# Three of four convolution chunks on TensorE in the first batch, with new planner lengths and ranks

## The reference, cut to what matters

```
x = x + 0.5 * ffn0(layernorm(x))      # shared weight plus 8 low-rank experts of rank 16
x = x + mamba2(layernorm(x) * w + b)
x = x + 0.5 * ffn0(layernorm(x))
x = x + 0.5 * moe(layernorm(x))       # 8 experts, top 2, and a shared expert of width 352
x = x + attention(layernorm(x))       # 16 heads of 8, linear attention over a batch
x = x + 0.5 * moe(layernorm(x))
```

```
xBC = u @ W_xbc.T                      # 512 channels: 256 of x, 128 of B, 128 of C
xBC = silu(conv4(xBC) + conv_b)        # each channel by itself, over time
```

## Time and profile before

| | |
|---|---|
| median of 3 runs | 946.68 us |
| lowest and highest | 939.96 and 947.03 us |
| the profiled execution, its own time | 947.6 us |
| span of that execution | 946.3 us |
| busy PE / PEld / DVE / ACT / POOL | 87 / 67 / 59 / 61 / 56 % |
| mean granted TensorE clock | 0.949 of full speed |

### The profile page before, as it was taken

One profiled execution on the slowest core, in us unless ns is written; L12 is line 12 of the kernel. 1 busy time (PEld: TensorE's weight loads), 2 busy tenths in 40 slices (PEclk: granted clock), 3 DMA queues, 4 the chain that ended last, 5 costly groups with the idle time before them and its releaser, 6 DMA issues.

```text
span 946.3 us, 15952 instructions
## 1 busy us (share of the span) xinstructions
PE 827.4 (87%) x4890; PEld 635.9 (67%) x4890; DVE 556.3 (59%) x1900; ACT 572.7 (61%) x1335; POOL 529.2 (56%) x648
## 2 busy tenths in 40 slices
PE   7999999999999987999789878987997895995983
PEld 6668688587776676686666667756666662764762
DVE  5487687877475757578546455598773461461113
ACT  4899787479877776786356335753743552552451
POOL 4058252586345787166753656565475665555453
PEclk9999998999999999999899899998997996998997
DMA  9920000010100012001131113121111421321323
GB/s 301 413 97 1 1 1 2 32 49 13 29 24 12 30 49 82 12 23 35 55 105 39 45 46 113 45 82 55 51 43 43 131 65 56 91 82 47 102 69 115
DMA packets 55652, 63.50 MB, mean 67 GB/s; under 512 B 7483, under 2 KB 47419, under 8 KB 55355
## 3 DMA queue, kind: packets, MB, share of 16 engines
q1 hardware_dynamic: 45299, 41.21, 14.2%
q0 software_dynamic: 9984, 20.60, 6.7%
q10 hardware_dynamic: 288, 0.67, 0.2%
HBM read 27.53 MB, written 34.92 MB: 66 GB/s over the span
## 4 chain that ended last, share of the span: by engine, by line
PE 48%; issue 14%; DVE 11%; POOL 11%; ACT 7%; DMA 6%; another core or an unknown queue 3%; SPq 0%; POOLq 0%; DVEq 0%; ACTq 0%
PE psum L529 8%; PE psum L800 7%; PE psum L820 6%; POOL sorted_x L1718 5%; PE psum L609 4%; PE psum L749 3%; PE psum L734 3%; PE psum L739 3%; DMA sent_y<-e_y,e_sx 2%; POOL sent_y L1728 2%; DMA e_sx<-sorted_x 2%; PE psum L678 2%; PE psum L842 2%; PE psum L524 1%
## 5 line engine op out<-in xcount | busy, mean ns | idle before, releaser
L1728 POOL DMA_INDIRECT sent_y<-e_y,e_sx x184 | 182.9, 994 | 156.1 <-ACT e_y L1557 111.4
L1718 POOL DMA_INDIRECT sorted_x<-g_xn,r_slot x128 | 129.0, 1008 | 38.6 <-issue 32.8
L800 PE MATMUL psum<-gu_w,e_sx 128*128 x368 | 129.4, 479 | 5.6 <-issue 3.5
L1252 DVE TENSOR_TENSOR e_h<-e_h,psum 128x352 f32<-128x352 f32 x96 | 47.8, 502 | 140.7 <-ACT e_h L1549 94.1
L820 PE MATMUL psum<-d_w,e_h 88*128 x736 | 104.5, 288 | 17.8 <-issue 13.7
L820 PEld LDWEIGHTS psum<-d_w,e_h 88*128 88x128 f32 x736 | 95.3, 200 | 34.8 <-issue 33.4
L1557 ACT ACTIVATE e_y<-psum,e_sx 128x128 f32<-128x128 f32 x184 | 57.5, 362 | 96.6 <-PE psum L820 57.2
L800 PEld LDWEIGHTS psum<-gu_w,e_sx 128*128 128x128 f32 x368 | 65.8, 197 | 34.9 <-issue 15.4
L1375 ACT ACTIVATE e_h<-psum 88x512 f32<-88x512 f32 x96 | 54.5, 572 | 48.0 <-PE psum L529 29.7
L1549 ACT ACTIVATE e_h<-psum 128x352 f32<-128x352 f32 x96 | 42.8, 450 | 62.5 <-PE psum L800 40.9
L529 PE MATMUL psum<-w_ffn,e_h 128*88 128x128 f32 x368 | 58.1, 283 | 20.8 <-issue 12.0
(11 more groups left out here) (241 smaller groups left out, 1933.0 us busy)
## 6 DMA issues: line engine op xcount, KB each, us to landing
e_sx<-sorted_x SPq DMA_DIRECT2D x88, 130.0 KB
sorted_x<-c_ys SPq DMA_DIRECT2D x8, 975.0 KB, 20.2
c_ys<-sent_y SPq DMA_DIRECT2D x14, 512.0 KB
sorted_x<-c_ys SPq DMA_DIRECT2D x8, 520.0 KB, 19.9
sent_y<-e_y,e_sx POOLq DMA_INDIRECT x184
xs<-in_x SPq DMA_DIRECT2D x8, 256.0 KB, 7.5
sorted_x<-g_xn,r_slot POOLq DMA_INDIRECT x128
out<-xs SPq DMA_DIRECT2D x7, 256.0 KB
```

The costliest lines, as they stand in the source:

```text
L800: last = e.matmul(two.banks[j].tile[:, 0:2 * IEXP], e_xT[k % SXS][:, j, :], gu_w[:, bass.ds(which[j] * (2 * IEXP), 2 * IEXP)], start=True, ...
L1718: e.indirect_dma_start(out=sorted_x[g], out_offset=bass.IndirectOffsetOnAxis(ap=r_slot[n][:, k, t:t + 1], axis=0), in_=rows[:, j, :], in_o ...
L1728: e.indirect_dma_start(out=sent_y[g], out_offset=bass.IndirectOffsetOnAxis(ap=e_sx[k % SXS][:, j, DM:DM + 1].bitcast(U32), axis=0), in_=e_ ...
```

## The change

Three things change together:

- `FOLDED` gets a third chunk for the first batch: chunks 1, 2 and 3 are folded there, and chunk 0 alone is tapped. The second batch stays as it was. `SCALED` follows and becomes (1, 2, 3), so one more DMA of 256 KB and one more multiplication on POOL prepare weights, and `w_gates` and the blocks of x behind it are loaded one place later in SP's queue.
- The planner counts a vector or scalar stage's engine as free 0.1 us earlier (`NEXT`), and thirteen lengths are replaced. For DVE all are shorter (for example the softplus series 3.67 to 2.8, taps 2.5 to 2.34); for POOL some are longer (the first half of four scatters 2.5 to 3.1, `finish` 1.29 to 1.6, two of `attn_out` 1.23 to 1.38); the issue of an expert load on SP 0.0 to 0.45.
- All rank lists are replaced.

```
-FOLDED = [(2, 3), (2, 3)]
+FOLDED = [(1, 2, 3), (2, 3)]
...
-FIRST = [177.82, 370.46, -25.93, -76.55, -165.11, 314.87, 71.46, 191.43]
+FIRST = [-1663.69, 1119.95, 260.62, 1433.81, -1495.37, 743.05, 409.58, 805.66]
...
-MAMBA = [-220.03, -96.33, 78.29, 264.38, -151.98, 471.11, 141.78, 20.16]
+MAMBA = [-1091.27, -162.89, 560.01, -466.1, -949.04, 507.42, 426.99, -1390.6]
...
-SORTED = [-32.7, 164.91, 159.92, 469.36, 679.99, 79.15, -248.93, 706.41]
-PAIRED = [114.03, 309.91, 329.73, 75.24, 663.43, 51.59, 642.15, 1319.33]
-PACE = [2.96, 5.27, 20.02, 6.49, 13.67, 17.1, 42.71, -15.01]
-SENDS = [576.11, 347.38, 560.08, 395.87, 1181.36, 460.83, 487.46, 1487.3]
+SORTED = [-580.11, -261.2, 560.37, -272.79, 299.31, -202.37, -1606.16, 1687.4]
+PAIRED = [220.41, 565.43, -75.92, -140.36, 1682.82, -653.42, 1054.59, 2350.85]
+PACE = [45.42, 98.75, 23.17, 108.81, -6.17, 12.68, 138.97, 28.74]
+SENDS = [236.06, 1496.96, 2345.51, -219.19, 999.47, 1264.13, 605.9, 1540.16]
...
-LATENCY, PE_LATENCY, TRANSFER, TABLE = 0.12, 0.25, 2.2, 1.3
+LATENCY, PE_LATENCY, TRANSFER, TABLE, NEXT = 0.12, 0.25, 2.2, 1.3, 0.1
...
-        free[name] = begin + course.cost
+        signals.now = begin + course.cost
+        free[name] = signals.now - (NEXT if name in ("vector", "scalar") else 0.0)
...
-                yield T + 14.0, 3.67, ("m_spexp", b + 1), ("a_exp", 1)
+                yield T + 14.0, 2.8, ("m_spexp", b + 1), ("a_exp", 1)
...
-                    yield T + 15.0 + TAP_STEP * n, 2.5, ("m_conv", k), ("m_tap", k + 1), ("m_halo_in", k + 1)
+                    yield T + 15.0 + TAP_STEP * n, 2.34, ("m_conv", k), ("m_tap", k + 1), ("m_halo_in", k + 1)
...
-                        yield (T + 8.0 + 4.0 * nth + 2.0 * half, 2.5, ("r_slot", g + 1), ("g_xn", i + 1), ("zeros", 16 * sum(EMPTY_LOADS)),
+                        yield (T + 8.0 + 4.0 * nth + 2.0 * half, 2.5 if half else 3.1, ("r_slot", g + 1), ("g_xn", i + 1), ("zeros", 16 * sum(EMPTY_LOADS)),
...
-                yield PAIR[g][t], 0.0, *scattered(g), before
+                yield PAIR[g][t], 0.45, *scattered(g), before
```

More of the change, by code:

```diff
@@ L87 @@
 ATANH = [2.0 / (2 * k + 1) for k in range(8)]
-FIRST = [177.82, 370.46, -25.93, -76.55, -165.11, 314.87, 71.46, 191.43]
-AGAIN = [135.09, -90.43, 35.89, -371.33, 70.69, 179.13, 111.78, 168.67]
-MAMBA = [-220.03, -96.33, 78.29, 264.38, -151.98, 471.11, 141.78, 20.16]
-CHUNK_AT = [24.78, 17.98, 107.37, 30.64, 119.59, 76.35, 60.04, 58.75]
+FIRST = [-1663.69, 1119.95, 260.62, 1433.81, -1495.37, 743.05, 409.58, 805.66]
+AGAIN = [775.72, -382.68, 554.79, -2296.04, -248.07, 248.47, 568.69, 223.34]
+MAMBA = [-1091.27, -162.89, 560.01, -466.1, -949.04, 507.42, 426.99, -1390.6]
+CHUNK_AT = [400.02, -213.35, 599.68, -252.35, -624.39, -851.15, 324.95, -1145.46]
 GAP = 4.9
@@ L277, in weave @@
             signals.late, free[name] = PE_LATENCY, clock.run(begin, course.cost)
-        signals.now = free[name]
+            signals.now = free[name]
         if not course.go_on():
@@ L790, in experts @@
                     numbers(g, 0)
-                yield T + 5.5, 1.28, ("two", 1), ("e_down", k - 1), ("w_late", 16 * 3), ("e_xT", k + 1)
+                yield T + 5.5, 1.21, ("two", 1), ("e_down", k - 1), ("w_late", 16 * 3), ("e_xT", k + 1)
                 on.wait_ge("w_late", 16 * 3)
@@ L981, in mamba @@
                 row = lambda k: dtt[:, k, :]
-                yield T, 1.8, ("f0_res", FFN0_AT[0, b] + 1), ("m_sum", b - 1)
+                yield T, 1.56, ("f0_res", FFN0_AT[0, b] + 1), ("m_sum", b - 1)
                 mv, veps, rstd, shifted, grown = m_ln_parts(m_ln[s])
@@ L988, in mamba @@
                 e.tensor_scalar(veps[:, 1, :], mv[:, :, 1], 1.0 + EPS, EPS * EPS, ALU.mult, ALU.add).then_inc(*S.up("m_var"))
-                yield T + 2.8, 0.4, ("m_rstd", b + 1)
+                yield T + 2.8, 0.25, ("m_rstd", b + 1)
                 on.wait_ge("m_rstd", b + 1)
@@ L1056, in chunk @@
                 e.tensor_tensor(gm, banks.tile("m_G", k)[:, 0:P], tri_incl[:, :], ALU.mult).then_inc(*S.up("m_gm"))
-                yield t + 2.5, 0.82, ("m_decay", k + 1), ("m_gm", k + 1)
+                yield t + 2.5, 0.7, ("m_decay", k + 1), ("m_gm", k + 1)
                 on.wait_ge("m_decay", k + 1)
@@ L1071, in chunk @@
                                     ALU.add).then_inc(*S.up("m_state"))
-                yield t + 6.0, 1.27, ("m_Y", k + 1), ("m_dx", k + 1)
+                yield t + 6.0, 1.22, ("m_Y", k + 1), ("m_dx", k + 1)
                 ybank = banks.tile("m_Y", k)
@@ L1113, in gates @@
                 shift(g_ln[s], "g_shift")
-                yield (T + 6.6, 2.8, ("g_logits", i + 1), ("w_gates", 16), ("c_add", START[max(g - 1, 0)]), ("r_rank", g - 1), ("g_exp", i - 1))
+                yield (T + 6.6, 2.67, ("g_logits", i + 1), ("w_gates", 16), ("c_add", START[max(g - 1, 0)]), ("r_rank", g - 1), ("g_exp", i - 1))
                 logits = banks.tile("g_logits", i)[:, 0:4 * GATES].rearrange("p (j e) -> p j e", e=GATES)
@@ L1674, in finish @@
                 T, rs = FINISH[b], m_rs[b % 2]
-                yield T + 0.5, 1.29, ("m_sq", 4 * b + 4), ("m_res", b - 1)
+                yield T + 0.5, 1.6, ("m_sq", 4 * b + 4), ("m_res", b - 1)
                 on.wait_ge("m_sq", 4 * b + 4)
@@ L1740, in attn_out @@
                 T, s, x = SECOND[b], b % 2, blk(b)
-                yield T, 1.23, ("k_q", b + 1), ("w_late", 16 * 3)
+                yield T, 1.38, ("k_q", b + 1), ("w_late", 16 * 3)
                 on.wait_ge("k_q", b + 1)
@@ L1744, in attn_out @@
                 e.tensor_tensor(x, x, p_b[:, :].unsqueeze(1).broadcast_to([P, 4, DM]), ALU.add).then_inc(*S.up("o_bias"))
-                yield T + 6.0, 1.23, ("o_div", b + 1)
+                yield T + 6.0, 1.38, ("o_div", b + 1)
                 on.wait_ge("o_div", b + 1)
```

10 lines of the change are left out of this document (5 added, 5 removed).

## The result

The kernel after takes 966.70 us (median of 4 runs, 963.66 to 969.23), the kernel before 946.86 beside it (939.96 to 951.22): ratio 1.030, 95% interval 1.026 to 1.034. That is 20 us slower; forecast were 935 us and a range up to 957. The profiled execution took 967.6 us with a span of 966.3, so it stands for the median.

A forecast was written before the change was run, and what follows sets the result against it. Order and latency were taken as the bound, not PE's sum, with ACT tightest early. From the profiled 947.6 us, -2 (convolution) and -10 (ranks) gave 935.6, against the median 934.7, said as 935; range 918 to 957 for 8 in 10.

The forecast's parts named there:

- Convolution, -2 us: First batch's four blocks: one chunk each from tapped to folded saves half of ACT's 5.3 us, less preparation; bounds -9.4, +10.3.
- all of this falls in the stretch with 32.5 us of idle time and fillers; I cost it at nothing: PE, 0 to 120 us: the folds' added 10.3 us are covered and cost nothing, at most 10.3 if uncovered.
- rival 3: First batch: new order fills the slack before 120 us, folds make PE the bound; 958 us; chance 0.02, plus 0.06 beyond 956.
- preparation +0.5, bounds 0 and +1.3: Start of kernel: longer scaling on POOL and one more 256 KB DMA delay what follows by 0.5 us.
- Half of ACT's 5.3 us as a gain: First batch: ACT loses 5.3 us of work and, nearly full for about half the stretch, gives -2.6 us.
- rival 4: Planner puts chunk 1's fold late, the recurrence waits longer, ACT's gain is eaten; about 945 us; chance 0.33 shared with rival 1.
- Page against trace: Whole kernel: 67% weight load busy would make the folds' 10.3 us free, 87% PE busy would not; weighed in between.
- Lengths, 0 us: Planner's replaced lengths change no instruction; their price by itself is nothing, they only tell what the ranks were fitted to.
- Ranks, -10 us: Of three late stretches (534-554, 776-800, 846-880 us), one gets other work beside its scatter run; three quarters of 13.9 us kept.
- rival 1: Whole kernel: new order neither better nor worse, only the convolution's 2 us gained; 945 us; chance 0.33 shared with rival 4.
- Rival 2: Second round of gates, sort, experts, after 700 us: one more scatter run falls on experts alone; +16.1 us, 962; chance 0.14.
- What would show it: Signs: record counts, ACT -5 us, early fillers -10; after 700 us less PE idle, higher clock, fewer unnamed waits; first sort's end.

The follow-up runs named there:

- e1: Kernel before, old order held by a list, chunk 1 of the first batch folded, old lengths: 960.58 us against 940.35, ratio 1.022.
- e5: Kernel before, TensorE projecting chunk 1 of the first batch's four blocks four times over, same result: 963.68 us against 951.18, ratio 1.0115.
- e6: Kernel before with the third set of fold weights prepared but unused: 957.83 us against 951.18, ratio 1.0043.
- e7: Kernel of e1 with only one of the four matmuls in chunk 1's fold: 973.55 us against the kernel before's 951.18, ratio 1.0138.
- e9: Kernel of e1 without the planner's condition that fold k waits for ACT applying fold k-2: 971.05 us against the kernel before's 949.59, ratio 1.0228.
- e2: Kernel after, order held, chunk 1 of the first batch tapped again: 971.0 us against the kernel before's 940.35, ratio 1.034.
- e4: New fold and new ranks with the old lengths, planned anew: 1009.45 us against the kernel before's 940.35, ratio 1.077.
- e8: Kernel after, order held, fillers sized at 1.0 of planned idle time, not 0.8: 981.92 us against the kernel before's 951.18, ratio 1.031.
- e17: Kernel after, unedited, beside the kernel before on a chip without unnamed ("remote") waits: 898.65 us against 898.33, ratio 1.0021.
- e11: Kernel before with the 128 scatters into sorted_x made plain DMAs to fixed places: 867.32 us against 949.59, ratio 0.914.
- e12: Kernel after with the plain scatters of e11: 901.50 us against the kernel before's 949.59, ratio 0.950.
- e14: Kernel before with two scratch fills on GpSimd after each of the 128 indirect scatters: 1072.23 us against 899.74, ratio 1.193.
- e16: Kernel before with only chunk 3 folded in the second batch, old lengths, ranks searched anew: 885.97 us against 899.74, ratio 0.985.
- e18: Repeat of e16 in another group of runs: 883.75 us against the kernel before's 898.33, ratio 0.985.
- e13: Kernel of e11 with a GpSimd scratch fill after each of the 128 plain DMAs: 928.26 us against the kernel before's 899.74, ratio 1.030.

## Why the prediction was wrong, point by point

**Convolution, -2 us.** In the old order the term was wrong by 22 us (e1, 20.4 in place of -2). Step "all of this falls in the stretch with 32.5 us of idle time and fillers; I cost it at nothing": measured 10.9 us (e5), the upper bound of 10.3 in full; it is also the price of rival 3. Step "preparation +0.5, bounds 0 and +1.3": 4.1 us with an interval of 0.7 to 7.6 (e6). Where they arise isn't shown: mamba's first normalising begins at 27.3 us in e6 and 24.8 in before, but at 26.2 both in e5, which prepares nothing more, and in e7, which prepares the third set too. The remainder, 5 us by e1 less e5 and e6 and 9 by e7 less e6, lies where a fold stands in PE's queue; 3 to 4.5 us of it are the fillers ahead of the third fold (e7, e9), locally. Half of ACT's 5.3 us as a gain: ACT's work fell by 3.4 us (e1) and 6.8 (after), and no run shows a gain from it. In the order of after the same fold shows no cost (e2: 1.034 without, 1.030 with), so there the term of -2 fits. That is luck: it rested on a cover that e5 refutes, and the ranks had been set for this fold, which I didn't count. Of rival 4, that the recurrence waits longer for the fold, nothing shows there either.

**Page against trace.** By the rows the 10.3 us would cost where there are no fillers; e5 shows that they cost even where there are. The Trainium skill, "Perfetto Trace Analysis", section "Identifying the Most-Contended Engine", calls weight load busy a better measure than matmul busy of how close TensorE is to its roofline. I had read out of the 67% that the 10.3 us would be free. The page doesn't say that, and e5 shows that it doesn't follow: far from the roofline, the added time was still on the path.

**Lengths, 0 us.** "The price by itself is nothing": they change the order as much as ranks do. Old lengths under the new ranks and the fold turn a ratio of 1.030 into 1.077 (e4).

**Ranks, -10 us.** This is the step that failed: "one of the three stretches gets other work beside its scatter run". In place of -10 the new order cost about 20 us with its fold, and 32 without (e2: 1.034, 1.026 to 1.041), on chips with late signals. The late stretches didn't go (after 700 us PE is idle for 51.7 of 266 us and the clock is 0.88, where 54.5 and 0.89 stood in the earlier trace rows); the unnamed waits on the chain after 700 us grew from 5.0 to 26.5 us, and 17 of the 20 us arise after the sixth scatter run. One more stretch came in at 269 to 297 us, 14 us of idle time plus busy time x (1 - granted clock), in all three profiles of this order that have late signals (after, e2, e8); it sets after back against e17, but by the third scatter run after is level with before. Where nothing is late the order of after is worth nothing, 0.2%, which was rival 1. That late signals make the difference is shown by one chip without them, and by the stalls on the chain; e11 and e12 don't fit it, so other causes beside it are not excluded.

**Rival 2** (a scatter run more that falls hard, 16.1 us, after 700 us, 962 us) had the price and the place nearly right and the condition wrong. I took it for a lack of work beside the scatter run. On the chip of e17 PE is busy for 23.9 of 24 us in the late run and 21.3 of 22 in the early one, so there was work enough. It stands still since the next instruction of its queue waits for a reader whose signal is late, as seen at 282 us. I had read the earlier trace rows, the 6.6 us of an unnamed wait, as a sign of little work, while in these stretches it goes with the loss itself.

**What would show it.** The counts of L609, L1032 and L1433 and ACT's relief came as said. ACT fell under 45 us in 50 to 100 us (40.95), but so it did in e5 (43.98) without any relief, so that sign tells nothing. "Fillers down ~10 with idle time unchanged" didn't come: they fell 4.9 (22.8 to 17.9) and idle time rose 2.2. Two of the three signs of a good order came in a kernel that was slower: idle time after 700 us under 54 us, and ACT's waits for the unnamed, 72.9 us against 82.6. "The first `sort` ending over 5 us later" was true: the first scatter starts at 205.1, 32.7 us later. It alone doesn't decide: e17 has it at 203.5 and loses nothing.

## What to carry to other kernels

Idle time and fillers are no cover for added work unless the work can be placed inside the gap; count it in full first, and make it prove otherwise. A wait for something that the trace can't name is a cost to be found before any order is judged, and it counts on the chain, not in its sum over the engines; an order that wins or loses 2% is run on more than one chip. In this kernel the lever is the scatter run: made longer it costs us for us (e14), made shorter it gives back a part (e11). Fewer folds in the second batch with ranks of their own won 1.5% (e16, e18).

## What the runs showed of the hardware

- The same program takes 895.0 or 966.3 us by the chip. The kernel before took 940 to 951 us in four groups of runs (that of the result included) and 898 to 900 in two; all traces from the first with indirect scatters have waits for "remote" (108 to 187 us in all), none from the latter has one.
- In a late stretch readers of PE's results go on together, 10 us and more after the matmuls were given out (292.16 and 292.21 us above). What delays them is open. Nearly all of it goes away with the indirect scatters (e11 10.5 us left, e12 14.4), and it occurs on some chips only (none in e13 to e18).
- 16 indirect DMAs of 128 rows take 20.8 us of POOL at the least (before, after, e17), 16 plain ones 10.4 (e11), small instructions between them included.
